# Expert stage in pairs of tiles with the weights stationary, and the one-hot columns by four comparisons

## The reference, cut to what matters

```
x = x + tanh(g_xattn) * xattn(layernorm(x), ctx)            # 4096 rows of 256
xf = layernorm(x)
routing = softmax(xf @ router_w.T)                          # 8 experts
top_w, top_i = top_k(routing, 2);  top_w = top_w / sum(top_w)
g = einsum('nd,ehd->neh', xf, w_gate)                       # 256 -> 512
u = einsum('nd,ehd->neh', xf, w_up)                         # 256 -> 512
h = silu(g) * u
y = einsum('neh,edh->ned', h, w_down)                       # 512 -> 256
x = x + tanh(g_ffn) * sum over the chosen experts of top_w * y
```

## Time and profile before

| what | value |
|---|---|
| median of 3 runs | 482.42 us (477.76 to 482.6) |
| profiled execution | 478.07 us, its span 476.2 us |
| TensorE busy | 422.5 us (89%), mean granted clock 0.909 |
| DVE / ACT / POOL busy | 239.4 / 192.2 / 242.1 us |
| DMA | 49.59 MB, mean 104 GB/s |
| chain that ended last | PE 77%, DVE 11% |

### The profile page before, as it was taken

The page is one execution under the profiler, slowest core; times in us unless marked ns, Lnnn a source line. Parts: engine busy times, 40 slices in busy tenths (PEclk is TensorE's granted clock), DMA queues, the critical chain, the costliest instruction groups (busy, mean ns, idle before and its releaser), DMA issues.

```text
span 476.2 us, 9017 instructions
## 1 busy us (share of the span) xinstructions
PE 422.5 (89%) x2491; PEld 356.2 (75%) x2492; DVE 239.4 (50%) x748; ACT 192.2 (40%) x480; POOL 242.1 (51%) x310
## 2 busy tenths in 40 slices
PE   7988886630669999999999999999999999999994
PEld 3847665420448888888888888888888898888884
DVE  3115899989935555555555543333333333333331
ACT  2353655302024555454545543343433333343331
POOL 8421676753053555265645555556554645555552
PEclk9595889555589999999999999999999999999999
DMA  6714566688521333833543334243333332423342
GB/s 196 234 46 133 192 214 219 211 284 274 210 70 22 49 67 49 305 55 57 105 124 60 56 56 66 47 67 51 62 55 57 48 63 45 67 45 56 56 66 27
DMA packets 31943, 49.59 MB, mean 104 GB/s; under 512 B 3516, under 2 KB 25489, under 8 KB 31921
## 3 DMA queue, kind: packets, MB, share of 16 engines
q0 software_dynamic: 13152, 18.65, 23.6%
q1 hardware_dynamic: 17511, 29.84, 18.6%
q10 hardware_dynamic: 1258, 0.84, 0.6%
HBM read 31.76 MB, written 17.57 MB: 104 GB/s over the span
## 4 chain that ended last, share of the span: by engine, by line
PE 77%; DVE 11%; DMA 3%; ACT 3%; issue 2%; POOL 2%; POOLq 0%; SPq 0%; ACTq 0%; DVEq 0%
PE GT L1088 19%; PE Y L1115 19%; PE UP L1088 19%; PE HT L1105 6%; PE S L997 4%; PE XT L1079 3%; PE O L1030 3%; DVE at_low L766 2%; DVE at_tile L877 2%; DMA out_rows<-y,idx 2%; ACT ex L559 1%; DVE xg L795 1%; DMA kr<-in_router 1%; DVE st L799 1%; PE O L1016 1%
## 5 line engine op out<-in xcount | busy, mean ns | idle before, releaser
L499 POOL DMA_INDIRECT out_rows<-y,idx x67 | 107.7, 1608 | 141.5 <-ACT y L625 90.2
L1115 PE MATMUL Y<-w_high,hT 128*128 x536 | 107.1, 283 | 0.0
L1088 PE MATMUL GT<-w_high,xtT 128*128 x272 | 102.7, 418 | 0.4 <-issue 0.4
L1088 PE MATMUL UP<-w_high,xtT 128*128 x272 | 102.0, 416 | 0.0
L930 DVE TENSOR_TENSOR hT<-HT,hT 128x512 fp32r<-128x512 f32 x67 | 46.4, 692 | 107.2 <-ACT hT L619 107.2
L491 POOL DMA_INDIRECT xt<-xn_rows,idx x71 | 70.9, 999 | 38.3 <-issue 20.7
L1115 PEld LDWEIGHTS Y<-w_high,hT 128*128 128x128 f32 x536 | 87.7, 190 | 3.0 <-issue 0.3
L625 ACT ACTIVATE y<-Y,xt 128x256 f32<-128x256 f32 x67 | 31.8, 474 | 139.8 <-PE Y L1115 114.3
L1115 PE MATMUL Y<-w_low,hT 128*128 x268 | 67.2, 283 | 0.0
L920 DVE TENSOR_TENSOR xtT<-XT,xtT 128x256 fp32r<-128x256 f32 x69 | 29.3, 425 | 59.6 <-ACT xtT L611 59.5
L1088 PEld LDWEIGHTS GT<-w_high,xtT 128*128 128x128 f32 x272 | 51.4, 189 | 10.3 <-issue 0.9
(11 more groups left out here) (158 smaller groups left out, 531.5 us busy)
## 6 DMA issues: line engine op xcount, KB each, us to landing
raw<-in_weights SPq DMA_DIRECT2D x16, 768.0 KB, 6.6
xn_rows<-pay SPq DMA_DIRECT2D x8, 528.0 KB, 3.2
xTg<-in_xT SPq DMA_DIRECT2D x8, 512.0 KB, 5.9
xg<-in_x SPq DMA_DIRECT2D x8, 512.0 KB, 5.1
out_rows<-xg SPq DMA_DIRECT2D x8, 512.0 KB, 3.3
xt<-xn_rows,idx POOLq DMA_INDIRECT x71, 2.8
out_rows<-y,idx POOLq DMA_INDIRECT x67, 3.8
kr<-in_ctx_rows SPq DMA_DIRECT2D x1, 308.0 KB
```

The costliest lines, as they stand in the source:

```text
L499: gp.indirect_dma_start(out=out, out_offset=bass.IndirectOffsetOnAxis(ap=idx[:, j:j + 1], axis=0), in_=y[:, j % 2, :], in_offset=None, com ...
L1088: last = mm(bank[:], xtT[:, s % 2, px, c * P:(c + 1) * P], parts[pw][c][:, bass.ds(e * HW + k * HID, HID)], start=(c == 0 and n == 0), sto ...
L1115: last = mm(Y[:, s % 2, 0:D], hT[:, px, c * P:(c + 1) * P], parts[pw][c // (HC // DC)][:, bass.ds(e * HW + DOWN + c % (HC // DC) * D, D)], ...
```

## The change

Two edits.

1. The expert stage goes by pairs of tiles (256 picks of one expert). The gate and up weights become the stationary operand and the transposed rows (256 columns) the moving one, so the hidden layer comes out with its hidden units on the partitions, as the down product needs it. The four HT transposes of a tile are gone. The weights' high and low parts are not kept for all experts: they are cut anew for each pair, from raw weights that all stay in memory: two halves `gu` (gate and up, 1024 elements each) and `dn` (down, 1024, two buffers). A pair's hidden layer is worked on in two halves q of 256 hidden units (512 elements each). The list has pairs: an expert's picks are filled up to a multiple of 256.
2. `at_tile` is made by four comparisons of 16 units each instead of 64 of one unit, and the tables are made behind `idx` instead of in front of it. The test for uneven experts and its branches are gone.

The order of a turn on each engine is in the diff. SP loads the experts' weights one group earlier (from the fifth group on), each as one transfer of 1.5 MB, and each waits until the one before has landed; experts 3 to 7 are issued behind the last group's store.

```diff
+PT = 2 * P
+PAIRS = (TOPK * N - NE) // PT + NE
+TILES = 2 * PAIRS
+CHUNK = 2 * CU
-XR = 8
-AHEAD = 6
+XR = 4
+AHEAD = 3
...
+            def load_weights(e):
+                if e > 0:
+                    sp.wait_ge(raw_loaded, 16 * e)
+                sp.dma_start(raw[:, e], weights[e].rearrange("p h n -> p (h n)")).then_inc(raw_loaded, 16)
...
-                if k >= GROUPS - EARLY:
-                    load_weights(k - (GROUPS - EARLY), raw_loaded if k == GROUPS - EARLY else raw_next)
+                if GROUPS // 2 <= k < GROUPS - 1:
+                    load_weights(k - GROUPS // 2)
             store_xn(GROUPS - 1)
+            for e in range(GROUPS // 2 - 1, NE):
+                load_weights(e)
...
+            for j in range(LEAST):                        # POOL
+                for t in range(2):
+                    add(j, t)
+                    gather(j + AHEAD, t)
...
+            def cut_gate_up(j, e, q):                     # ACT
+                act.wait_ge(up_ready, 2 * j + q - 1)
+                nc.scalar.copy(gu[:, 0, q], gate_up_of(e, q)).then_inc(gu_high[q], 1)
+            def cut_down(j, e, b):
+                act.wait_ge(down_ready, 2 * j - 2 + DOWN0)
+                nc.scalar.copy(dn[:, 0, b], down_of(e)).then_inc(dn_high, 1)
+            def weigh(j, s, e):
+                for t in range(2):
+                    act.wait_ge(y_added, 32 * j + 16 * t - 16 + Y_ADDED0)
+                    act.wait_ge(down_ready, 2 * j + t + 1 + DOWN0)
+                    nc.scalar.mul(y[:, t], Y[:, t, 0:D], xt[:, 2 * s + t, bass.ds(e + CW, 1)]).then_inc(y_ready, 1)
...
+            def turn(j, s, i, e=None, behind=2):          # ACT
+                    e1 = weights_of(j + 1)
+                    act.wait_ge(raw_loaded, 16 * e1 + 16)
+                    cut_gate_up(j + 1, e1, 0)
+                hid_highs(j, 0)
+                silu(j, 1)
+                    tile_highs(j + 2, s % 2)
+                hid_highs(j, 1)
+                    silu(j + 1, 0)
+                    cut_gate_up(j + 1, e1, 1)
+                    cut_down(j + 1, e1, (s + 1) % 2)
+                weigh(j, s, e)
...
-            for u in range(UNITS):
-                last = ts(at_tile[:, u], iota_t[:], col[:, u:u + 1], None, ALU.is_equal)
-                if u % CU == CU - 1:
-                    last.then_inc(tile_hot, 1)
+            for c in range(0, UNITS, CHUNK):
+                tt(out=at_tile[:, c:c + CHUNK], in0=iota_t[:].unsqueeze(1).to_broadcast([P, CHUNK, TILES]),
+                   in1=col[:, c:c + CHUNK].unsqueeze(2).to_broadcast([P, CHUNK, TILES]),
+                   op=ALU.is_equal).then_inc(tile_hot, 1)
...
+            def low_of(out, whole, high):                 # DVE
+                return tt(out=out, in0=whole, in1=high.bitcast(F32), op=ALU.subtract)
+            def turn(j, s, i, e=None, behind=2):
+                gate_up(j, 0)
+                    e1 = weights_of(j + 1)
+                    cut_gate_up(j + 1, e1, 0)
+                hid_lows(j, 0)
+                gate_up(j, 1)
+                    tile_lows(j + 2, s % 2)
+                hid_lows(j, 1)
+                    cut_gate_up(j + 1, e1, 1)
+                    cut_down(j + 1, e1, (s + 1) % 2)
...
+            def first_layer(bank, b, q, w):               # TensorE
+                for h in range(2):
+                    for c in range(DC):
+                        for n, (px, pw) in enumerate(HI_LO):
+                            last = mm(bank[:, h * PT:(h + 1) * PT], gu[:, pw, q, c, w, h * P:(h + 1) * P], xtT[:, b, px, c],
+                                      start=(c == 0 and n == 0), stop=(c == DC - 1 and n == 2))
+            def gate(j, b, q):
+                pe.wait_ge(gu_low[q], j + 1)
+                pe.wait_ge(silu_ready, 2 * j + q - 1 + SILU0)
+                first_layer(GT[:, q], b, q, 0).then_inc(gate_ready, 1)
+            def turn(j, s, i, none=None, behind=2):
+                b = s % 2
+                gate(j, b, 1)
+                up(j, b, 1)
+                    transpose_pair(j + 2, (s + 2) % XR, i + (s + 2) // XR)
+                    pe.wait_ge(x_low, j + 2)
+                    gate(j + 1, 1 - b, 0)
+                down(j, b)
+                    up(j + 1, 1 - b, 0)
```

More of the change, by code:

```diff
@@ L290, in rows, with gate_up_of, down_of, each_pair @@
             return xg[:, slot_of(g) + t]
[L292 to L296, removed]
+        def gate_up_of(e, q):
+            return raw[:, bass.ds(e, 1), :].rearrange("p e (h n) -> p (e h) n", h=HALVES)[:, :, 0:DOWN].rearrange(
+                "p h (w n) -> p h w n", w=2)[:, :, :, q * HALF:(q + 1) * HALF]
+        def down_of(e):
+            return raw[:, bass.ds(e, 1), :].rearrange("p e (h n) -> p (e h) n", h=HALVES)[:, :, DOWN:HW]
+        def each_pair(eng, turn):
+            with eng.Fori(0, LEAST // XR) as i:
+                carried = None
+                for s in range(XR):
+                    carried = turn(XR * i + s, s, i, carried)
+            used = eng.value_load(pairs_used[:], min_val=LEAST, max_val=PAIRS)
+            def rest(j, carried):
+                if j < PAIRS:
                     with eng.If(used > j):
-                        tile(j)
-                        rest(j + 1)
-            rest(TURNS * XR)
+                        rest(j + 1, turn(j, j % XR, j // XR, carried, PAIRS - 1 - j))
+            rest(LEAST, None)
             return used
@@ L508, in _, with rest @@
             for j in range(AHEAD):
[L509 to L514, removed]
+                for t in range(2):
+                    gather(j, t)
+            for j in range(LEAST):
+                for t in range(2):
+                    add(j, t)
+                    gather(j + AHEAD, t)
+            used = pool.value_load(pairs_used[:], min_val=LEAST, max_val=PAIRS)
+            def rest(j):
+                if j < PAIRS:
+                    with pool.If(used > j):
+                        for t in range(2):
+                            add(j, t)
+                            if j + AHEAD < PAIRS:
+                                gather(j + AHEAD, t)
+                        rest(j + 1)
+            rest(LEAST)
         @block.scalar
@@ L593, in _ @@
                     copy_expT(k + 2)
[L595 to L619, removed]
+            def weights_of(j):
+                return act.value_load(pair_expert[0:1, bass.ds(j, 1)], min_val=0, max_val=NE - 1)
@@ L638, in _ @@
+            act.sem_inc(passed_act)
+            for q in range(2):
+                nc.scalar.copy(gu[:, 0, q], gate_up_of(e, q)).then_inc(gu_high[q], 1)
+            nc.scalar.copy(dn[:, 0, 0], down_of(e)).then_inc(dn_high, 1)
             tile_highs(0, 0)
@@ L904, in _ @@
             stt(out=idx[:], in0=size[:], scalar=-1.0, in1=shift[:], op0=ALU.add, op1=ALU.add).then_inc(idx_ready, 1)
-            def cut_low(e, h, at, size):
-                return tt(out=w_low[h][:, bass.ds(e * HW + at, size)],
-                          in0=raw[h][:, bass.ds(e, 1), at:at + size].rearrange("p e n -> p (e n)"),
-                          in1=w_high[h][:, bass.ds(e * HW + at, size)].bitcast(F32), op=ALU.subtract)
-            def cut_all_low(e):
-                dve.wait_ge(weight_high, e + 1)
-                for h in range(HALVES):
-                    cut_low(e, h, 0, HW)
@@ L932, in _ @@
-            is_skewed = dve.value_load(skewed[:], min_val=0, max_val=1)
-            with dve.If(is_skewed == 1):
-                for e in range(1, NE):
-                    cut_all_low(e)
+            after(mark(tt(out=past[:], in0=J[:].unsqueeze(2).to_broadcast([1, PAIRS, NE]),
+                          in1=cum[0:1, :].unsqueeze(1).to_broadcast([1, PAIRS, NE]), op=ALU.is_ge)))
+            after(mark(v.tensor_reduce(tex[:], past[:], axis=AX.X, op=ALU.add)))
+            ts(pairs_used[:], cum[0:1, NE - 1:NE], 0.5, None, ALU.mult)
@@ L966, in _ @@
+            each_pair(dve, turn)
         @block.tensor
@@ L1066, in _ @@
             pe.wait_ge(low_ready, GROUPS)
-            for k in range(GROUPS):
-                pe.wait_ge(tile_hot, k + 1)
-                for u in range(k * CU, (k + 1) * CU):
-                    last = mm(L[:, LIST:LIST + TW], at_low[:, u], at_tile[:, u], start=(u == 0), stop=(u == UNITS - 1))
+            for c in range(UNITS // CHUNK):
+                pe.wait_ge(tile_hot, c + 1)
+                for u in range(c * CHUNK, (c + 1) * CHUNK):
+                    last = mm(L[:, LIST:LIST + TILES], at_low[:, u], at_tile[:, u], start=(u == 0), stop=(u == UNITS - 1))
@@ L1085, in first_layer @@
-            def first_layer(bank, s, e, k):
-                for c in range(DC):
-                    for n, (px, pw) in enumerate(HI_LO):
-                        last = mm(bank[:], xtT[:, s % 2, px, c * P:(c + 1) * P],
-                                  parts[pw][c][:, bass.ds(e * HW + k * HID, HID)],
-                                  start=(c == 0 and n == 0), stop=(c == DC - 1 and n == 2))
-                return last
-            def gate(j, s, e):
```

(58 more changed lines are left out.)

361 lines of the change are left out of this document (135 added, 226 removed).

## The result

The changed kernel takes 732.88 us (median of 4 runs, 727.21 to 736.84) against 482.51 us for the kernel before. The ratio is 1.534, with a 95% interval of 1.522 to 1.545. I had forecast 469.5. The profiled execution took 734.98 us, with a span of 732.8.

The account below looks back on a forecast made before the run. The chain of adds was expected to replace TensorE as bound: first add 151, 67 steps of 4.65 = 311.5, landing 3.8, end 1.3, span 467.6; with 1.9 more, 469.5 us. Range 458 to 484.

Parts of the forecast that it names:

- the chain of adds: Adds to out_rows, each waiting for the last landing: expected new bound, 9.3 us per pair, bounds 9.1 and 9.45.
- In between stands one gather, as before: On POOL, between a pair's two adds of 4.57 us each: one gather, counted within the 9.1 us.
- The timetable of the turn: Expert loop laid out from gate(j,1) at 0: XT at 2.9, end at 9.0 us, slack 0.5 to 0.9 us.
- the four rivals: Four outcomes for the expert loop: 460 us (chance 0.2), 463 to 475 (0.5), 489 (0.12) and 482 (0.18).
- the list of what would be wrong for all: Wide DVE or ACT instructions on strided weights slower than 1.22 and 1.05 us, or a first add far from 151.
- C: Rival: both adds of a pair meet a two-operand DVE instruction, 4.94 us per add, 489 us; chance 0.12.
- The first gathers: Ahead of the loop: gathers beside the expert weight loads land later, charged 2.4 us.
- The two-operand DVE instructions: In the loop: adds on POOL starting while DVE reads two SBUF operands take 1.86 us instead of 1.59.
- TensorE's 9.0 us per pair: TensorE's work per pair in the expert loop: 9.0 us against 2 x 4.87 = 9.74 before.
- rival A: In the loop TensorE still sets the pace and the adds fit under it at 4.5 us each: 460 us; chance 0.2.

Follow-up runs that it names:

- the run at the full clock: The changed kernel with 18 extra, unused matmuls in front of each XT wait; 673.21 us, ratio 1.403.
- SP holds the weights back: The version with the early counters, with SP's loads of experts 5 to 7 waiting for the first three gathered pairs; 469.45 us, ratio 0.961.
- the run with the old order: The version with the early counters, with an add waiting first for y, then for the landing, as in the kernel before; 481.54 us, ratio 1.009.
- the run with 36 extra matmuls: The changed kernel with 36 extra, unused matmuls in front of each XT wait; 753.9 us, ratio 1.574.
- the version with the early counters: Changed kernel, both gathers ahead of a turn's adds, SP's five starting counter increments ahead of the loads of experts 3 to 7; 462.42 us, ratio 0.961.
- the gathers first alone: The changed kernel with POOL issuing both gathers of a turn ahead of its two adds; 473.39 us, ratio 0.983.

## Why the prediction was wrong, point by point

**The step that failed** is one clause on the chain of adds: "In between stands one gather, as before". I priced that gather for the adds and never asked who waits for it. The timetable of the turn put XT at 2.9 us without looking at its data, so a wait that sets the pace was put at nothing. It could have been worked out from the kernel's order and the same rows. Gathers went six tiles ahead before and three pairs now, which is as many rows but half as many turns, and XT still runs two turns ahead. What is left is one: XT(j+2) stands in turn j and its second gather behind the second add of pair j-1. In the timetable pair j-1 is weighed just before turn j starts. Its second add follows 4.1 us later as measured (4.57 by rows 6), the gather 1.9 behind that, the landing 2.8 behind the gather: 8.8 us into the turn, against 2.9. A turn of 9.0 made longer by these 5.9 us is 14.9, which is what the run at the full clock shows, and with the low clock behind the gap it is 17.0. In the kernel before the gather stood behind the add of tile j-4. Two runs show it: 732.9 to 473.4 by the lead given back, 482 to 839 by the lead taken away. The clock that fell in the gap is part of it, 68 us of the loss in the loop. None of the four rivals named it, and neither did the list of what would be wrong for all. C, the slow one, had another mechanism and 489 us.

**SP's order** was the second thing passed over. I named the loads' traffic as a cost of the start, and not that the increments of five counters stand behind those loads. In the changed kernel the first gate waited 6.3 us for them, and the first add came at 159.5, not at 151.

**The first gathers** beside the weights' traffic were charged 2.4 us. From idx to the first XT it took 138.04 - 128.89 = 9.2 us in the changed kernel, and 5.4 where SP holds the weights back. So the traffic cost 3.8 us, and the term was too small by over a third.

**The chain of adds** as the new bound was wrong for this kernel, by a size read from a kernel with another order of waits: 4.57 where 4.16 holds. The mechanism was right, that the adds can bound the loop, as the run with the old order shows: with it the chain runs at 9.66 us per pair, a little above my bound of 9.45, and sets the pace.

**The two-operand DVE instructions** hold up POOL as read from the earlier trace rows. In the run with 36 extra matmuls a gather started 1.03 us before such an instruction ended (403.17 + 1.23 - 403.37), and took 0.91 us more than its 0.99:

```profile
403.17 1.23 DVE L900 TENSOR_TENSOR gu<-raw,gu 128x1024 fp32r<-128x1024 f32 x1 [0.60 <-ACT gu L609]
...
403.37 1.90 POOL L486 DMA_INDIRECT xt<-xn_rows,idx  x1 [0.30 <-issue]
```

In the version with the early counters it falls on the second gather of a pair (1.3 to 1.9 us). The next add starts 0.3 us behind that gather, but no wait of TensorE in the loop follows from it, so it costs nothing there.

**What held** is TensorE's 9.0 us per pair (9.07), 34 pairs, and the durations: cutting 1024 elements 1.04 us on ACT and 1.22 on DVE for 1.05 and 1.22, 0.62 and 0.68 for a half, at_tile 5.56 for 5.7. With the lead and the counters mended, the loop runs as rival A had it: TensorE sets the pace, and the adds just fit: 4.1 us within a pair and 5.0 to the next one, with two gathers in between, are 9.1, as long as TensorE's turn. A gave 460 us, and that version takes 462, but this agreement is in part luck. In its profile the first add stands at 143.35, not at A's 151, and the 67 steps take 306.7 us, not 301.5.

## What to carry to other kernels

When the size of a work item doubles, count the lead of each prefetch again, in turns of the consumer and not in buffers. Then look at what stands ahead of the prefetch on its own queue: a load that is issued behind a result's store or add is only as early as that result. Idle time that such a late load makes on TensorE can cost more than its length, since the clock fell with it here (0.80 granted, and 1.00 with the gap filled). And an increment, or a wait, has a place in its queue like any other instruction. Look there before pricing durations.

## What the runs showed that I had not expected

- The order of two waits in front of an indirect DMA on POOL is worth some 0.5 us for each one that a landing releases: about 4.6 us with the landing waited for last, in either kernel, and about 4.1 with it waited for first. Why is open, as the traces show only the steps.
- The attention stage, whose code up to the weight loads is the same in all these kernels, does not take the same time in every execution: idx came at 119.0 us in the profiled execution of the version with the early counters and at 129.6 in that with the gathers first alone. The granted clock between 40 and 80 us was 0.89 in the first and 0.75 in the second. So a distance of 10 us between two profiles says little on this kernel. The first of these took 456.9 us, against a median of 462.4.
